# Attention: two of the eight rectangular chunks subtract their maxima by an accumulating transfer

## What is computed

```python
Q = (x @ Wq + bq).reshape(b, s, H, C) * inv_sqrt_c        # H = 16 heads, C = 64 channels
K = (x @ Wk + bk).reshape(b, s, H, C)
V = (x @ Wv + bv).reshape(b, s, H, C)
scores = jnp.einsum('bshq,bshk->bshqk', Q, K)              # outer product per token and head
mask = jnp.triu(jnp.ones((C, C), dtype=bool), 1)
scores = jnp.where(mask, -inf, scores)
w = jax.nn.softmax(scores, axis=-1)
attn = jnp.einsum('bshqk,bshk->bshq', w, V)
return attn.reshape(b, s, HID) @ Wo + bo
```

## Time and profile before

| | |
|---|---|
| median of 3 runs | 3993.14 us (3992.79 to 3994.1) |
| span of the profiled execution | 3993.6 us |
| PE, DVE, ACT, POOL busy | 89%, 82%, 49%, 84% of the span |
| attention stage (from the first subtraction at 1047.9 us) | 2945.7 us, 32 tiles |
| one tile, repeating | about 91.8 us |

### The profile page before, as it was taken

One profiled execution on the slowest core, in us unless ns is written; L12 is line 12 of the kernel. 1 busy time (PEld: TensorE's weight loads), 2 busy tenths in 40 slices (PEclk: granted clock), 3 DMA queues, 4 the chain that ended last, 5 costly groups with the idle time before them and its releaser, 6 DMA issues.

```text
span 3993.6 us, 72415 instructions
## 1 busy us (share of the span) xinstructions
PE 3555.5 (89%) x26059; PEld 3107.7 (78%) x26059; DVE 3278.4 (82%) x3459; ACT 1974.7 (49%) x2535; POOL 3344.8 (84%) x1502
## 2 busy tenths in 40 slices
PE   5593699977599999999999999999999999999999
PEld 4252688866388888888888888888888888888888
DVE  8536555547699999899999999998999999999988
ACT  1010233344265555655555565555555555655555
POOL 1678455541699999999999999999999999999997
PEclk8696899998799999999999999999999999999999
DMA  9322456669000000000000000000000000000000
GB/s 381 110 103 77 143 181 191 187 211 335 15 5 5 8 5 5 5 5 5 5 5 6 6 5 8 5 5 5 5 5 6 5 5 6 5 8 5 5 5 5
DMA packets 110620, 209.18 MB, mean 52 GB/s; under 512 B 16608, under 2 KB 77280, under 8 KB 110304
## 3 DMA queue, kind: packets, MB, share of 16 engines
q1 hardware_dynamic: 84192, 140.90, 11.0%
q0 software_dynamic: 21504, 59.93, 4.1%
q10 hardware_dynamic: 4608, 4.20, 0.3%
HBM read 183.34 MB, written 107.74 MB: 73 GB/s over the span
## 4 chain that ended last, share of the span: by engine, by line
PE 58%; DVE 7%; issue 4%; ACT 2%; POOL 2%; DVEq 0%; ACTq 0%; DMA 0%; POOLq 0%
PE at_num L1483 21%; PE at_den L1483 19%; PE at_work L1461 9%; PE at_work L1471 4%; DVE at_pv L1169 2%; PE at_misc L1509 2%; POOL at_s L1250 2%; DVE at_k_low L1396 2%; PE at_misc L1515 2%; ACT at_s L1329 1%; DVE at_s L1169 1%; PE at_work L1462 1%; DVE at_k_top L1393 1%; DVE at_pv L1170 1%; ACT at_k_far L1270 1%
## 5 line engine op out<-in xcount | busy, mean ns | idle before, releaser
L1250 POOL TENSOR_TENSOR at_s<-at_s,at_m 128x2048 f32<-128x2048 f32 (+7 forms) x768 | 2511.3, 3306 | 31.0 <-DVE at_s L1169 22.9
L1329 ACT ACTIVATE at_s<-at_s 128x2048 f32<-128x2048 f32 (+7 forms) x768 | 1080.7, 1418 | 611.5 <-POOL at_s L1250 611.2
L1483 PE MATMUL at_den<-k_ident,at_s 128*128 128x128 f32 x9216 | 1135.2, 273 | 54.0 <-ACT at_s L1329 52.5
L1483 PE MATMUL at_num<-k_ident,at_pv 128*128 128x128 f32 x9216 | 1142.8, 274 | 0.5 <-DVE at_pv L1170 0.5
L1483 PEld LDWEIGHTS at_num<-k_ident,at_pv 128*128 128x128 f32 x9216 | 1049.9, 142 | 91.2 <-issue 69.3
L1483 PEld LDWEIGHTS at_den<-k_ident,at_s 128*128 128x128 f32 x9216 | 1037.0, 141 | 85.7 <-ACT at_s L1329 60.0
L1170 DVE TENSOR_TENSOR at_pv<-at_s,at_vp 128x2048 f32<-128x2048 f32 (+7 forms) x512 | 692.1, 1352 | 229.9 <-ACT at_vp L1304 179.9
L1170 DVE TENSOR_TENSOR at_s<-at_q,at_kp 128x2048 f32<-128x2048 f32 (+7 forms) x512 | 691.6, 1351 | 14.2 <-ACT at_kp L1299 9.4
L1169 DVE TENSOR_TENSOR at_pv<-at_s,at_vp 128x2048 f32<-128x2048 f32 x256 | 584.8, 2284 | 0.0
L1169 DVE TENSOR_TENSOR at_s<-at_q,at_kp 128x2048 f32<-128x2048 f32 x256 | 582.1, 2274 | 0.0
L1461 PE MATMUL at_work<-k_region,at_xT 128*128 128x512 f32 x788 | 408.2, 644 | 105.6 <-ACT at_k_far L1270 81.7
(11 more groups left out here) (235 smaller groups left out, 3557.7 us busy)
## 6 DMA issues: line engine op xcount, KB each, us to landing
moe_w<-experts SPq DMA_DIRECT2D x256, 384.0 KB
slot_x<-k_region SPq DMA_DIRECT2D x16, 2144.0 KB, 25.2
moe_x<-slot_x SPq DMA_DIRECT2D x256, 134.0 KB, 3.3
cmb_y<-picked SPq DMA_DIRECT2D x32, 768.0 KB, 8.5
at_xT<-xT SPq DMA_DIRECT2D x33, 128.0 KB, 2.2
e_x<-u SPq DMA_DIRECT2D x4, 1024.0 KB, 9.5
picked<-moe_yo,moe_row POOLq DMA_INDIRECT x256, 3.2
xT<-cmb_xT ACTq DMA_DIRECT2D x32, 128.0 KB, 5.9
```

What stands on the lines that cost most here:

```text
L1250: nc.gpsimd.tensor_tensor(part(s_slot, c), part(s_slot, c), by_query(m[unit_of(c)][:], c), ALU.subtract).then_inc(sub_done, 1)
L1329: nc.scalar.activation(part(s_slot, c), part(s_slot, c), ACT.Exp, scale=C ** -0.5).then_inc(exp_done, 1)
L1483: ins = nc.tensor.matmul(dst[:, b * P:(b + 1) * P], buf[:, at:at + P], k.ident[:], start=(c in (0, NTRI) and x == 0 and b == 0), stop=Fals ...
```

## The change

In chunks 9 and 13 of every tile (`BY_DMA`), POOL no longer subtracts. It issues a transfer from `m` into the chunk's slot that adds what it moves to what is there, and since a sum is wanted, `m` now holds the negated maximum (the last step of `maxima` takes `fall - m` in place of `m - fall`), and the other chunks add it. Each of the two chunks has a semaphore of its own, on which the exponential waits; the counts on `sub_done` are renumbered for 22 in place of 24 chunks (`subtracted`). Ahead of each transfer POOL increments a semaphore that nobody waits for (`settle`).

```diff
+BY_DMA = (9, 13)
+        dma_done = {c: a.sem(f"dma_done{c}") for c in BY_DMA}
+        issued = a.sem("issued")
+        def subtracted(t, c):
+            return t * (NCH - len(BY_DMA)) + sum(b not in BY_DMA for b in range(c + 1))
...
-                        nc.gpsimd.tensor_tensor(m[h][:, 0:HALF], m[h][:, 0:HALF], fall[:], ALU.subtract
+                        nc.gpsimd.tensor_tensor(m[h][:, 0:HALF], fall[:], m[h][:, 0:HALF], ALU.subtract
...
-                        nc.gpsimd.tensor_tensor(part(s_slot, c), part(s_slot, c), by_query(m[unit_of(c)][:], c),
-                                                ALU.subtract).then_inc(sub_done, 1)
+                        if c in BY_DMA:
+                            settle(pool, issued)
+                            nc.gpsimd.dma_start(part(s_slot, c), by_query(m[unit_of(c)][:], c), accum_op=ALU.add
+                                                ).then_inc(dma_done[c], 16)
+                        else:
+                            nc.gpsimd.tensor_tensor(part(s_slot, c), part(s_slot, c), by_query(m[unit_of(c)][:], c),
+                                                    ALU.add).then_inc(sub_done, 1)
...
+                    past_sub = subtracted(t - 1, (NCH if h else NTRI) - 1)
-                    wait(act, sub_done, past)
+                    wait(act, sub_done, past_sub)
...
-                        act.wait_ge(sub_done, count(t, c))
+                        if c in BY_DMA:
+                            act.wait_ge(dma_done[c], t * 16 + 16)
+                        else:
+                            act.wait_ge(sub_done, subtracted(t, c))
```

## The result

| | kernel before | changed kernel |
|---|---|---|
| median of 20 runs | 3993.22 us (3989.99 to 3994.93) | 3999.05 us (3994.86 to 4004.71) |
| ratio, 95% interval | | 1.0015 (1.0008 to 1.0022) |
| span of the profiled execution | 3993.6 us | 3994.2 us |

The change makes the kernel slower by 0.15%. That is inside the 0.2% that the forecast called no change, yet beyond the interval: a small real loss where none was forecast. The profiled execution was one of the shorter ones, so the trace is read for where time goes within a tile, and the loss as a whole is taken from the medians.

A forecast was written before the change was run, and what follows sets the result against it. A PE, ACT, DVE, ACT loop of 91.8 us per tile, without POOL, was taken to bound the kernel. With nothing on it moved, 0 x 32, the forecast was the median, 3993 us; range 3949 to near 4110.

The forecast's parts named there:

- What bounds the kernel: Tile-to-tile loop: 47.3 (PE) + 2.5 (ACT) + 41.3 (DVE) + 0.7 (ACT) = 91.8 us, with no POOL instruction in it.
- What the change takes away: Two POOL subtractions, 9.1 us per tile, 291 us in all less the issues; worth nothing on the path setting the end.
- L: Time from POOL's turn to the transfer's last byte landed, in chunks 9 and 13; taken as 8.7 us.
- the upper end of the range: For the transfer's time: three passes 12.1 us, or 13 us and beyond if the issue grows with the pieces.
- The cover: How long chunk 9's and 13's transfers may take before PE, DVE or ACT's later work is late.
- The limits of 8.8, 10.2 and 9.3 us: Transfer times beyond which PE's chunk 9 sum, DVE's need of that exponential, and DVE's product 16 are late.
- The step that failed: Reversed subtraction, additions, counters and `settle` on POOL cost nothing that shows, in an engine with some 7 us to spare.
- A second step: The sum over tiles: with L at 8.7 us nothing on the loop moves, 0 x 32.
- Rival (b): PE's clock stays up before chunk 11 if chunk 9's lateness splits its standing: 3949 to 3985 us, say 3960; chance 0.17.
- 34 at L = 9.7: Gain in us from PE's clock staying up before chunk 11, from 1.7 - (L - 9.4) in 26 tiles.
- Rival (a): Chunk 9's cover runs out, DVE losing L - 10.2 per tile and PE waiting at chunk 13: 4079 to 4163; chance 0.38.
- The range: Whole kernel's time from 3949, the clock's full gain, to near 4110, at L = 12.4; leaves out about 0.12.

The follow-up runs named there:

- e5: Changed kernel with neither subtraction nor transfer in chunks 9 and 13 (result not the reference's): 3992.91 us, ratio 1.0006.
- e6a: Kernel before, with ACT copying v for the tile's first half after chunk 0's exponential in place of chunk 1's: 3935.66 us, ratio 0.9863.
- d3: Changed kernel with three spare additions of 128x512 on GpSimd ahead of each transfer, delaying its issue: 4039.1 us, ratio 1.0126.
- e3: Changed kernel, but in the first tile GpSimd adds chunks 9 and 13 as before, without transfers: 3994.79 us, ratio 1.001.
- e1: Changed kernel with ACT's wait for PE's projection put last, on the copy of q itself: 3992.16 us, ratio 1.001.
- e2: Changed kernel's counts and semaphores without its transfers; GpSimd adds the negated maxima in chunks 9 and 13 itself: 3994.75 us, ratio 1.001.
- d1: Changed kernel with one spare addition of 128x512 on GpSimd ahead of each transfer, delaying its issue: 3981.85 us, ratio 0.9983.
- e6b: Changed kernel with v for the tile's first half copied after chunk 0's exponential in place of chunk 1's: 3914.86 us, ratio 0.9815.
- f1: The changed kernel itself, run again as a control: 3994.22 us, ratio 1.0012.
- f2: Changed kernel with v copied early and ACT's wait for PE put on the copy of q: 3915.03 us, ratio 0.9809.
- f4: Changed kernel with v copied early and the transfer in chunk 9 alone, chunk 13 added by GpSimd: 3915.21 us, ratio 0.9811.

## Why the prediction was right or wrong

*What bounds the kernel*: right. The loop PE, ACT, DVE, ACT of 91.8 us passes by POOL; e5 takes both subtractions away and gains nothing, and e6a, which touches the loop alone, gains 1.4%.

*What the change takes away*: right in kind. POOL was relieved of 9.1 us per tile less its issues and stands for DVE instead.

*L*: 8.7 us was taken, with two passes and an issue that doesn't grow with the pieces. Measured are 8.2 us from POOL's turn and 7.8 from the issue, in the first tile 9.5. The issue takes 1.29 us for 512 pieces, against 0.96 for the 128 rows of another kind of transfer; the upper end of the range, four times as much, is refuted. The fit of the Trainium skill (DMA: Bandwidth & Descriptors), doubled for two source reads, gave 6.8 us; the trace has 7.8, so the measurement decides. The two source reads of the Trainium skill (Collectives: The Full Stack, The bandwidth ceiling) agree with q0's 6.1 us per transfer against 3 for one pass.

*The cover*: right for the repeating tile. The limits of 8.8, 10.2 and 9.3 us were confirmed by d3 within 0.1 us. In the first tile DVE's limit was 8.0 us.

*The step that failed* is the sentence that the counters and the `settle` cost nothing that shows, because these are semaphore instructions in an engine, POOL, that would have time to spare. The counts are read by ACT, and there, behind the wait for PE, on the loop, the renumbering put a register operation: 0.07 us x 31 = 2.2 us. The prediction had listed the engines in the loop and looked at the new counts only where they are raised. A second step failed beside it: the sum was made for one steady tile and multiplied by 32, and the first tile, where the transfer lands after 9.5 us and DVE's cover ends at 8.0, loses 1.6 us (e3). Together 3.8 us. A third part comes through the clock: the rounds grow from 5 or 6 tiles to mostly 7, which makes the mean loop longer by 0.11 to 0.12 us and not by 0.07, and adds some 1.4 us over 31 tiles (table behind e5). That the longer loop is what lengthens the rounds is shown by e1 (transfers, short rounds) against e2 and e5 (no transfers, long rounds). The three parts make 5.2 us; the medians show 5.8 and, on the other chip, 2.8, and the intervals of both contain 5.2.

The forecast of the time as "3993 within 8 us" held, but that is no credit to the step: it put at nothing three small costs that happen to add up to less than its own margin.

*Rival (b)*: the mechanism is right, at the wrong length. L = 8.2 fell short of the 9.4 that it asked for, so it played no part in the changed kernel; d1 and e6b show it. Its "34 at L = 9.7" should be 36 by its own formula (26 x 1.4), which changes nothing. *Rival (a)*: limits right, but not reached in the repeating tile; the first tile's 1.5 us of DVE is this rival on a small scale.

*The range* of 3949 to 4110 held the time; its upper part paid for a fourfold issue that didn't come.

## What to carry to other kernels

An engine that is 84% busy can be off the loop altogether: find the loop by laying the engines' timelines side by side, and relieve an engine only after the standing in the loop has been taken away; one constant on the loop (v copied before q) brought 1.4%, and then the transfer in chunk 9 another 0.5%. A new semaphore or a changed count is to be followed to every engine that waits for it: where two waits shared a register value and no longer do, look at which instruction carries the wait for the late partner, and put that wait last. And count the first tile by itself: its cover is thinner, and a transfer's time there has to be read there.

## What the runs showed of the hardware

An accumulating transfer between two places of SBUF, 128 partitions x 4 pieces of 2 KB, keeps the 16 engines busy for 6.1 us (173 GB/s) and lands 7.8 us after its issue. The longest of 64 took 9.5 us (9.4 in e1, f1, e6b, f2 and f4); it was the first one, at whose end 24 KB of instructions were fetched.

PE's standing before chunk 11, of 2.1 to 2.4 us, costs a further 1.7 us through the clock in most tiles and nothing in others, and the same standing can do either; which it does comes in rounds, and a loop 0.07 us longer made the rounds a tile or two longer. Split into some 0.5 and 1.7 us the standing left the clock up in 29 of 31 tiles (e6b), 29 of 32 (f2) and 31 of 32 (f4). Delaying an instruction that another engine waits for made the kernel faster (d1): where a standing can't be avoided, its place still has a price.
